# Turning the edge counts for the mask with transposing DMAs in place of GpSimd copies and TensorE products

## The chip, the cores and the metric

One core of a Trainium2 chip. The metric is device time in microseconds for one launch of the whole program, median of several runs. The kernel is written by hand with explicit semaphores: each engine (TensorE = PE, VectorE = DVE, ScalarE = ACT, GpSimd = POOL, SyncE = SP, which here only issues DMAs) runs its instructions in the written order and waits on semaphores.

## The reference

Two graph layers over 1024 nodes with 768 features and 16384 edges, each followed by a residual and a layer norm. The first is a graph attention network (8 heads, then 1 head), the second a two-step graph convolution. What the change touches belongs to the attention:

```
h = (x @ W1).reshape(n, 8, 768)                  # 1024 x 6144
alpha_s, alpha_d = h . a_src, h . a_dst          # per node and head
e = leaky_relu(alpha_s[src] + alpha_d[dst], 0.2)
m = segment_max(e, dst)                          # over the edges that arrive at dst
e = exp(e - m[dst]); alpha = e / (segment_sum(e, dst)[dst] + 1e-16)
out = segment_sum(h[src] * alpha, dst)           # then elu, a second such layer, and so on
```

The kernel is dense: it builds a matrix of edge counts `count[src, dst]` once and works with 1024x1024 matrices. For the maximum over arriving edges it needs a mask with the destination on the partitions: 0 where there is an edge, a large number where there is none.

## The kernel before

The layer's big product x @ W1 runs in 96 steps. QN = 12 column blocks q of 512 columns, each of NB = 8 node blocks b of 128 rows; step (q, b) has number n = 8q + b. A step is 18 products of TensorE (six blocks of features, each with three products of float32 split in a high and a low part, lines L41 to L43, moving 512 columns) into bank n % 6 of the PSUM. Banks 6 and 7 serve small work. Around a step (n):

- ACT copies the bank as the high part into `st[n % 4]` (L623, `main_high`). Before, it waits that the DMA which saved `st[n % 4]` four steps ago has landed (`h_saved`).
- DVE forms two logit sums from the bank (L979) and the low part of `st` (L1074), which counts `main_lo` up. TensorE's step n + 6 waits for `main_lo` of step n, since it takes the same bank.
- SP waits for `main_lo` and saves `st` to HBM (L445, 512 KB).
- ACT casts one block of the next W1 column block (`weights_high`, L591, in steps b = 1 to 6), POOL forms its low part `wl` (L574); TensorE's step (q + 1, 0) waits for all six.
- At b = 0 SP loads the weights of block q + 2 (L369, 1.5 MB), at b = 1 the vectors `a_bc` of block q + 1 (L373), each broadcast over the partitions.

The counts lie in `countT`, int16, [128 partitions of src, 8 blocks of src, 1024 dst], and are complete at the start of block q = 5. Then the mask is made, one block m of 128 destinations at a time, m = 0 to 7, two of them in each of q = 5, 6, 7, 8 (`BLOCK_AT` and `MASK_AT`):

- POOL copies `countT[:, :, block m]` to `staged[m % 2]` as bf16 (L570), two blocks ahead of its work on `wl` for that q. From m = 2 it waits for `staged_turned`.
- TensorE, after step (q, 1) for even m and (q, 5) for odd m, multiplies the eight 128x128 parts of `staged` with the unit matrix `ident_b`: the parts turned, in banks 6 and 7 (L1557). It waits for `staged_done` and for the mask before (`mask_done`), as the two banks are used again.
- ACT, after its work of step (q, 3) or (q, 7), waits for `staged_turned` and makes the mask by two Relu instructions that read banks 6 and 7 (L671).
- SP, one step later, saves that block of the mask to HBM (L377); DVE reads masks 0 to 3 for the first maxima after step (7, 1).

In the same stage SP handles vectors of logits and exponents: `row_bc` (L381), `expo_scratch` (L387, written as single values of 4 bytes) and `expo_bc` (L394). All the DMAs named here but a few small ones at the program's start run on SP's one hardware queue and its 16 DMA engines, in the order in which SP issues them. From q = 12 on the program goes to the attention sums (TensorE again in L41 to L43, `psum<-ph,hc`), the second layer, and the convolution.

Of the kernel before, what the change touches and what calls it, by code (L numbers as in the profile page):

```python
# [8 lines left out]
I16 = mybir.dt.int16  # L9
# [111 lines left out]
def graph_and_layers(nc, sem, put, psum, banks, t):  # L121
# [24 lines left out]
    junk = put("junk", 155648, [P, 2, CW], BF16)  # L146
    a_bc = [put(f"a_bc{i}", 157696 + 4096 * i, [P, 2, CW], F32) for i in range(2)]

    staged = [put(f"staged{i}", 165888 + 2048 * i, [P, NB, P], BF16) for i in range(2)]
    lane_sums = put("lane_sums", 169984, [P, N], F32)  # L150
    ident_b = put("ident_b", 179200, [P, P], BF16)
    mask_late = put("mask_late", 174080, [P, 2, N], BF16)
# [100 lines left out]
    count_full, count_out = sem("count_full"), sem("count_out")  # L253
    cols_full, cols_done = sem("cols_full"), sem("cols_done")
    x_turned, x_hi, x_lo = sem("x_turned"), sem("x_hi"), sem("x_lo")
    staged_done, staged_turned, deg_sum, mask_done = sem("staged_done"), sem("staged_turned"), sem("deg_sum"), sem("mask_done")
    mask_out = [sem(f"mask_out{i}") for i in range(2)]
    deg_step, root_done, dinv_done = sem("deg_step"), sem("root_done"), sem("dinv_done")
    dinvT_full, dinvT_done, dinv_out, many_full, many_done = (sem(n) for n in ("dinvT_full", "dinvT_done", "dinv_out", "many_full", "many_done"))
# [105 lines left out]
    with nc.Block() as block:  # L365
        @block.sync
        def _(sp):
# [7 lines left out]
            def save_mask(b):  # L375
                sp.wait_ge(mask_done, 2 * b + 2)
                sp.dma_start(mask_d[:, b * N:(b + 1) * N], mask_of(b)).then_inc(mask_out[b % 2], 16)  # L377

            def load_row(v):
                h = v % H  # L380
                sp.dma_start(row_bc[:, :], logits_d[h * NB:(h + 1) * NB, :].rearrange("b p -> (b p)").partition_broadcast(P)).then_inc(row_in, 16)  # L381
# [40 lines left out]
            for q in range(QN):  # L422
                for b in range(NB):
                    n = q * NB + b
                    if 1 <= q < QN - 1 and b == 1:
                        sp.wait_ge(part_sum, parts_before[q * NB])
                        load_vectors(q + 1)
                    if q < QN - 2 and b == 0:
                        if q == 0:
                            sp.wait_ge(w0_lo, FB)  # L430
                        else:
                            sp.wait_ge(w_lo, FB * q)
                        load_weights(q + 2)
                    if q == QN - 1 and b in (1, 2, 3):
                        if b == 1:
                            sp.wait_ge(staged_turned, NB)
                            sp.wait_ge(deg_sum, DEG_PARTS + 1)
                            for i in range(2):
                                sp.wait_ge(mask_out[i], 16 * NB // 2)
                        load_nodes(b - 1)  # L440
                    if n == STEPS - 1:
                        spread_exponents(1)
                    sp.wait_ge(main_lo, n + 1)
                    g = q * 4
                    sp.dma_start(h_d[g:g + 4, :, b, :, :].rearrange("g p k c -> p g k c"), st[n % 4][:, :, :, :].bitcast(F32)).then_inc(h_saved[n % 4], 16)  # L445
                    if (q, b - 1) in MASK_AT:
                        save_mask(MASK_AT[(q, b - 1)])
                    if b == 0 and (q - 1, NB - 1) in MASK_AT:
                        save_mask(MASK_AT[(q - 1, NB - 1)])
                    if (q, b) in SAVE_AT:  # L450
                        save_logits(SAVE_AT[(q, b)])
                    if (q, b) == (5, 1):
                        sp.wait_ge(count_out, NW)
                        sp.wait_ge(logits_out, 16)
                        load_row(0)
                    if (q, b) == (7, 4):
                        save_exponents(0)
                        load_row(1)
                    if (q, b) == (7, 7):
                        spread_exponents(0)  # L460
                    if (q, b) == (8, 4):
                        save_exponents(1)
                    if (q, b) == (10, 0):
                        sp.wait_ge(logits_out, 32)
                        load_row(2)
                    if (q, b) == (10, 4):
                        sp.wait_ge(dinvT_done, 1)
                        sp.dma_start(dinv_d, dinvT[:, :]).then_inc(dinv_out, 16)
# [77 lines left out]
        def _(pool):  # L546
# [9 lines left out]
            for q in range(QN - 1):  # L556
                if q in (2, 3):
                    pool.wait_ge(count_out, 8 * (q - 1))
                    for w in range(8 * (q - 2), 8 * (q - 1)):
                        pool.sem_clear(hot_ready[w % HOT_SEMS]).then_inc(hot_cleared, 1)  # L560
                        pool.sem_clear(hot_free[w % HOT_SEMS]).then_inc(hot_cleared, 1)
                if q == QM:
                    pool.wait_ge(count_out, NW)
                    for done in hot_ready + hot_free:
                        pool.sem_clear(done)
                for b in (2 * (q - QM), 2 * (q - QM) + 1):
                    if 0 <= b < NB:
                        if b >= 2:
                            pool.wait_ge(staged_turned, b - 1)
                        nc.gpsimd.tensor_copy(staged[b % 2][:, :, :], countT[:, :, b * P:(b + 1) * P]).then_inc(staged_done, 1)  # L570
                i = (q + 1) % 2
                for f in range(FB):
                    pool.wait_ge(w_hi, FB * (q + 1) + f + 1)
                    nc.gpsimd.tensor_tensor(wl[i][:, f, :], wr[i][:, f, :], wh[i][:, f, :].bitcast(F32), ALU.subtract).then_inc(w_lo, 1)  # L574
# [13 lines left out]
        def _(act):  # L588
# [54 lines left out]
            for q in range(QN):  # L643
                for b in range(NB):
# [18 lines left out]
                        weights_high(q + 1, b - 1)  # L663
                    if (q, b) in MASK_AT:
                        m = MASK_AT[(q, b)]
                        act.wait_ge(staged_turned, m + 1)
                        act.wait_ge(const_c, 3)
                        if m >= HNB + 2:
                            act.wait_ge(mask_out[m % 2], 16 * (m // 2))
                        for i in range(2):  # L670
                            nc.scalar.activation(mask_of(m)[:, i * 512:(i + 1) * 512], banks[6 + i][:, :], ACT.Relu, bias=unlinked[:, 0:1],  # L671
                                                 scale=NOT_LINKED).then_inc(mask_done, 1)
                    if (q, b) == (9, 6):
                        act.wait_ge(deg_step, 3)
# [786 lines left out]
        def _(pe):  # L1461
# [57 lines left out]
            for q in range(QN):  # L1519
                if q >= 1:  # L1520
                    pe.wait_ge(w_lo, FB * q)
                for b in range(NB):
# [23 lines left out]
                    if n + 1 in COUNT_AFTER:  # L1546
                        w = COUNT_AFTER[n + 1]
                        pairs = pe.value_load(range_i[w:w + 1, 1:2], min_val=FIRM // 2 + 1, max_val=EP)
                    if (q, b) in BLOCK_AT:
                        m = BLOCK_AT[(q, b)]  # L1550
                        pe.wait_ge(staged_done, m + 1)
                        if m == 0:
                            pe.wait_ge(logitT_done, 1)
                        else:
                            pe.wait_ge(mask_done, 2 * m)
                        for s in range(NB):
                            last = nc.tensor.matmul(banks[6 + s // 4][:, (s % 4) * P:(s % 4 + 1) * P], staged[m % 2][:, s, :], ident_b[:, :],  # L1557
                                                    start=True, stop=True)
                        last.then_inc(staged_turned, 1)
                    if (q, b) == (9, 0):  # L1560
                        pe.wait_ge(mask_done, 2 * NB)
                        pe.wait_ge(deg_sum, DEG_PARTS)
# [628 lines left out]
```

## Time and profile before

| | us |
|---|---|
| median of 3 runs | 1658.85 (1658.64 to 1658.88) |
| the profiled execution, its own time | 1656.4 |
| its span, first to last instruction | 1654.6 |
| PE busy | 1630.6 (99%), 7552 products |
| DVE busy | 1234.6 (75%) |
| ACT busy | 770.0 (47%) |
| POOL busy | 155.7 (9%) |
| SP's queue, share of 16 DMA engines | 52.9%, 267 MB |
| granted TensorE clock | 0.997 |

The profile is of one execution. "Busy" is the union of the instructions of an engine; a product of TensorE is shown as lasting 0.39 us though the next one starts 0.227 us after it, since they overlap in the array, so that starts are to be read, not lengths. SP's rows (SPq) are the times in which it issues a DMA, not the transfer; the transfer ends at its "landing". The stage of the change, q = 5 to 8, lies between 214 and 349 us of the span.

### The profile page before, as it was taken

The numbers are of one execution on the slowest core, as the hardware profiler recorded it, in microseconds if no ns is written. First come the engines' busy times: TensorE is split into PE (matmuls) and PEld (weight loads), VectorE is DVE, ScalarE is ACT, GpSimd is POOL, SyncE is SP. The second block draws the span as 40 slices with busy tenths as digits, with TensorE's granted clock in tenths as the row PEclk, the third lists the DMA queues.
The fourth block names the chain that finished last, engine by engine and source line by source line (L and its number), as shares of the span: only waits on it lengthen the run. The fifth ranks groups of instructions, "written<-read, shape, count | busy, mean of one in ns | idle before, by whom it ended". The sixth has DMA issues, their size and how long they took to land. (4 is left out here: it accounts for less than half of the span.)

```text
span 1654.6 us, 21905 instructions
## 1 busy us (share of the span) xinstructions
PE 1630.6 (99%) x7552; PEld 1368.2 (83%) x7552; DVE 1234.6 (75%) x2442; ACT 770.0 (47%) x1231; POOL 155.7 (9%) x126
## 2 busy tenths in 40 slices
PE   7999999999999999999999999999999999999998
PEld 6878888888878888888888888888888888989898
DVE  7877667655988788788778788877886668785447
ACT  3222223222565565456555555655564435644340
POOL 1211232322200000000000000000000001031003
PEclk9999999999999999999999999999999999999999
DMA  7444555984647475558647565754754447023222
GB/s 258 161 156 156 162 193 190 242 214 151 223 172 184 170 210 153 131 188 226 155 152 200 156 167 187 200 143 164 200 140 172 178 163 195 21 94 97 66 96 88
DMA packets 135331, 271.86 MB, mean 164 GB/s; under 512 B 24234, under 2 KB 83508, under 8 KB 122676
## 3 DMA queue, kind: packets, MB, share of 16 engines
q1 hardware_dynamic: 133968, 267.26, 52.9%
q0 software_dynamic: 1152, 3.15, 1.0%
q8 instruction: 63, 1.03, 0.3%
q14 instruction: 48, 0.39, 0.1%
q10 hardware_dynamic: 100, 0.03, 0.0%
HBM read 210.01 MB, written 60.40 MB: 163 GB/s over the span
## 5 line engine op out<-in xcount | busy, mean ns | idle before, releaser
L41 PE MATMUL psum<-ph,hc 128*128 128x512 f32 x768 | 299.4, 390 | 2.2 <-DVE pl L1040 1.2
L42 PE MATMUL psum<-pl,hc 128*128 128x512 f32 x768 | 298.8, 389 | 0.0
L43 PE MATMUL psum<-ph,hc 128*128 128x512 f32 x768 | 298.8, 389 | 0.0
L41 PE MATMUL psum<-wh,xTh 128*128 128x512 f32 x570 | 226.3, 397 | 0.4 <-issue 0.4
L42 PE MATMUL psum<-wl,xTh 128*128 128x512 f32 x570 | 222.2, 390 | 0.0
L43 PE MATMUL psum<-wh,xTl 128*128 128x512 f32 x570 | 222.0, 389 | 0.0
L979 DVE CUSTOM_DVE_ANT_0 junk<-psum,a_bc 128x512 bf16<-128x512 f32 (+1 forms) x256 | 129.8, 554 | 118.6 <-ACT st L623 108.6
L623 ACT CAST st<-psum 128x512 fp32r<-128x512 f32 x96 | 56.4, 588 | 296.2 <-PE psum L43 285.3
L41 PEld LDWEIGHTS psum<-ph,hc 128*128 128x128 f32 x768 | 144.2, 188 | 33.9 <-DVE pl L1040 2.1
L43 PEld LDWEIGHTS psum<-ph,hc 128*128 128x128 f32 x768 | 144.2, 188 | 30.0
L42 PEld LDWEIGHTS psum<-pl,hc 128*128 128x128 f32 x768 | 144.2, 188 | 29.7
L695 ACT ACTIVATE he<-mean,bias 128x512 f32<-128x512 f32 x96 | 69.6, 725 | 210.7 <-DVE mean L1129 210.7
L43 PE MATMUL psum<-w2h,hl 128*128 128x512 f32 x384 | 149.5, 389 | 0.0
L41 PE MATMUL psum<-w2h,hh 128*128 128x512 f32 x384 | 149.5, 389 | 0.0
L42 PE MATMUL psum<-w2l,hh 128*128 128x512 f32 x384 | 149.4, 389 | 0.0
L43 PEld LDWEIGHTS psum<-wh,xTl 128*128 128x128 f32 x570 | 107.0, 188 | 22.8
L41 PEld LDWEIGHTS psum<-wh,xTh 128*128 128x128 f32 x570 | 107.1, 188 | 22.2 <-issue 0.6
L42 PEld LDWEIGHTS psum<-wl,xTh 128*128 128x128 f32 x570 | 107.2, 188 | 20.8
L1129 DVE TENSOR_TENSOR mean<-psum,rden 128x512 f32<-128x512 f32 x96 | 65.8, 686 | 69.9 <-PE psum L43 69.8
L574 POOL TENSOR_TENSOR wl<-wr,wh 128x512 fp32r<-128x512 f32 x66 | 87.4, 1324 | 316.6 <-ACT wh L591 316.6
L687 ACT CAST w2h<-w2r 128x768 fp32r<-128x768 f32 x96 | 79.6, 829 | 73.4 <-PE psum L43 73.4
L641 ACT CAST ph<-pf 128x512 fp32r<-128x512 f32 x128 | 79.7, 622 | 70.1 <-DVE pf L1035 70.1
(285 smaller groups left out, 3116.7 us busy)
## 6 DMA issues: line engine op xcount, KB each, us to landing
hc<-h_scratch SPq DMA_DIRECT2D x96, 1024.0 KB, 5.3
h_scratch<-st SPq DMA_DIRECT2D x96, 512.0 KB, 3.2
w2r<-in_L_gnn_W SPq DMA_DIRECT2D x96, 384.0 KB, 6.8
wr<-in_L_gnn_W SPq DMA_DIRECT2D x12, 1536.0 KB, 8.6
gwr<-in_L_gnn_W SPq DMA_DIRECT2D x24, 384.0 KB, 3.4
row_bc<-logits_scratch SPq DMA_DIRECT2D x16, 512.0 KB, 12.9
expo_bc<-expo_scratch SPq DMA_DIRECT2D x16, 512.0 KB, 6.2
xr<-in_x SPq DMA_DIRECT2D x2, 1536.0 KB, 10.2
```

Of the source, the lines that this page charges most:

```text
L41: nc.tensor.matmul(out, sh, mh, start=first, stop=False, skip_group_check=not grouped)
L42: nc.tensor.matmul(out, sh, ml, start=False, stop=False, skip_group_check=not grouped)
L43: return nc.tensor.matmul(out, sl, mh, start=False, stop=last, skip_group_check=not grouped)
L574: nc.gpsimd.tensor_tensor(wl[i][:, f, :], wr[i][:, f, :], wh[i][:, f, :].bitcast(F32), ALU.subtract).then_inc(w_lo, 1)
L623: nc.scalar.copy(st[n % 4][:, :, 0, :], banks[n % 6][:, :].rearrange("p (g c) -> p g c", g=4)).then_inc(main_hi, 1)
L641: nc.scalar.copy(ph[v % 2][:, i, :], pf[:, i % 2, :]).then_inc(p_hi, 1)
L687: nc.scalar.copy(w2h[:, g % 3, :], w2r[:, g % 3, :]).then_inc(w2_hi, 1)
L695: nc.scalar.activation(he[:, g % 2, :], mean[:, g % 2, :], ACT.Exp, bias=b)
L979: nc.vector.tensor_tensor_reduce(out=junk[:, s % 2, 0:hi - lo], in0=banks[n % 6][:, lo:hi], in1=a_bc[q % 2][:, k, lo:hi], scale=1.0, scala ...
L1129: nc.vector.tensor_tensor(mean[:, g % 2, :], banks[6 + g % 2][:, :], rden[:, :], ALU.mult).then_inc(a_out, 1)
```

## The change

The turning is done by DMAs. After SP has issued the save of step (q, 1) or (q, 5) it issues eight transposing DMAs for block m, each of one 128x128 part of `countT` of 2-byte integers, straight from `countT` into `staged[m % 2]`, which is int16 now. The first batch waits for the last counts (`count_out`); from m = 2 a batch waits for the mask that last read this `staged`. The batch stands ahead of everything that SP had after that save. ACT waits for the landing of all eight (a semaphore for each of the two buffers) and reads `staged` in place of banks 6 and 7. POOL's eight copies and TensorE's 64 products are gone.

```diff
-    staged = [put(f"staged{i}", 165888 + 2048 * i, [P, NB, P], BF16) for i in range(2)]
+    staged = [put(f"staged{i}", 165888 + 2048 * i, [P, NB, P], I16) for i in range(2)]
...
-    staged_done, staged_turned, deg_sum, mask_done = sem("staged_done"), sem("staged_turned"), sem("deg_sum"), sem("mask_done")
+    staged_turned = [sem(f"staged_turned{i}") for i in range(2)]
+    deg_sum, mask_done = sem("deg_sum"), sem("mask_done")
...
+            def turn_counts(m):
+                if m == 0:
+                    sp.wait_ge(count_out, NW)
+                elif m >= 2:
+                    sp.wait_ge(mask_done, 2 * (m - 1))
+                for s in range(NB):
+                    sp.dma_start(staged[m % 2][:, s, :], countT[:, s, m * P:(m + 1) * P], transpose=True).then_inc(staged_turned[m % 2], 16)
...
-                            sp.wait_ge(staged_turned, NB)
+                            sp.wait_ge(mask_done, 2 * NB)
...
                     sp.dma_start(h_d[g:g + 4, :, b, :, :].rearrange("g p k c -> p g k c"), st[n % 4][:, :, :, :].bitcast(F32)).then_inc(h_saved[n % 4], 16)
+                    if (q, b) in BLOCK_AT:
+                        turn_counts(BLOCK_AT[(q, b)])
...
-                for b in (2 * (q - QM), 2 * (q - QM) + 1):
-                    if 0 <= b < NB:
-                        if b >= 2:
-                            pool.wait_ge(staged_turned, b - 1)
-                        nc.gpsimd.tensor_copy(staged[b % 2][:, :, :], countT[:, :, b * P:(b + 1) * P]).then_inc(staged_done, 1)
...
-                        act.wait_ge(staged_turned, m + 1)
+                        act.wait_ge(staged_turned[m % 2], 16 * NB * (m // 2 + 1))
...
-                            nc.scalar.activation(mask_of(m)[:, i * 512:(i + 1) * 512], banks[6 + i][:, :], ACT.Relu, bias=unlinked[:, 0:1],
+                            nc.scalar.activation(mask_of(m)[:, i * 512:(i + 1) * 512], staged[m % 2][:, 4 * i:4 * i + 4, :].rearrange("p s n -> p (s n)"), ACT.Relu, bias=unlinked[:, 0:1],
...
-                    if (q, b) in BLOCK_AT:
-                        m = BLOCK_AT[(q, b)]
-                        pe.wait_ge(staged_done, m + 1)
-                        if m == 0:
-                            pe.wait_ge(logitT_done, 1)
-                        else:
-                            pe.wait_ge(mask_done, 2 * m)
-                        for s in range(NB):
-                            last = nc.tensor.matmul(banks[6 + s // 4][:, (s % 4) * P:(s % 4 + 1) * P], staged[m % 2][:, s, :], ident_b[:, :],
-                                                    start=True, stop=True)
-                        last.then_inc(staged_turned, 1)
```

TensorE between step (5, 1) and step (5, 2), before (`wh_71` and `wl_73` are the high and low part of the weights):

```order
1142 L43 MATMUL psum<-wh_71,xTl 128x512
1143 L1557 MATMUL psum<-ident_b,staged_84 128x128 [waits logitT_done,staged_done]
1144 L1557 MATMUL psum<-ident_b,staged_84 128x128 x7
1145 L41 MATMUL psum<-wh_71,xTh 128x512 [waits main_lo]
1146 L42 MATMUL psum<-wl_73,xTh 128x512
```

And after, at the same place:

```order
1141 L42 MATMUL psum<-wl_73,xTh 128x512
1142 L43 MATMUL psum<-wh_71,xTl 128x512
1143 L41 MATMUL psum<-wh_71,xTh 128x512 [waits main_lo]
1144 L42 MATMUL psum<-wl_73,xTh 128x512
1145 L43 MATMUL psum<-wh_71,xTl 128x512
```

The two rows with `ident_b` and their waits have gone from between the steps; nothing has taken their place.

SP's queue from the save of step (5, 1) on, before:

```order
69 L445 DMA h_scratch<-st_78 128x4x256 [waits main_lo]
70 L381 DMA row_bc<-logits_scratch 128x1024 [waits logits_out,count_out]
71 L445 DMA h_scratch<-st_79 128x4x256 [waits main_lo]
72 L445 DMA h_scratch<-st_80 128x4x256 [waits main_lo]
73 L445 DMA h_scratch<-st_77 128x4x256 [waits main_lo]
74 L377 DMA mask_scratch<-mask_half 128x1024 [waits mask_done]
```

And after:

```order
69 L454 DMA h_scratch<-st_78 128x4x256 [waits main_lo]
70 L386 DMA_TRANSPOSE staged_84<-countT 128x128 [waits count_out]
71 L386 DMA_TRANSPOSE staged_84<-countT 128x128 x7
72 L390 DMA row_bc<-logits_scratch 128x1024 [waits logits_out,count_out]
73 L454 DMA h_scratch<-st_79 128x4x256 [waits main_lo]
74 L454 DMA h_scratch<-st_80 128x4x256 [waits main_lo]
```

Eight transposing DMAs stand behind the save of step (5, 1) and ahead of the load of `row_bc` and of the saves of the next steps.

ACT at step (5, 3), before:

```order
123 L623 CAST st_80<-psum 128x4x128 [waits h_saved3,main_full]
124 L591 CAST wh_70<-wr_68 128x512 [waits w_in0]
125 L671 ACTIVATE mask_half<-psum,unlinked 128x512 [waits const_c,staged_turned]
126 L671 ACTIVATE mask_half<-psum,unlinked 128x512
127 L623 CAST st_77<-psum 128x4x128 [waits h_saved0,main_full]
```

And after:

```order
123 L629 CAST st_80<-psum 128x4x128 [waits h_saved3,main_full]
124 L597 CAST wh_70<-wr_68 128x512 [waits w_in0]
125 L677 ACTIVATE mask_half<-staged_84,unlinked 128x512 [waits const_c,staged_turned0]
126 L677 ACTIVATE mask_half<-staged_84,unlinked 128x512
127 L629 CAST st_77<-psum 128x4x128 [waits h_saved0,main_full]
```

The mask stands where it stood, between the same neighbours; it waits for a landing now and reads `staged`.

## Rows read from the trace of the kernel before

**Rows 1.** The page's first part: busy us, share of the span, instructions
```profile
PE 1630.6 (99%) x7552; PEld 1368.2 (83%) x7552; DVE 1234.6 (75%) x2442; ACT 770.0 (47%) x1231; POOL 155.7 (9%) x126
```

**Rows 2.** Waits of PE, whole span: waited for, us in total, times, longest
```profile
PE psum L1465 <- DVE key_f L897: 5.0, 1, 5.0
PE psum L1533 <- ACT wh L591: 3.9, 1, 3.9
...
PE psum L41 <- DVE pl L1040: 1.2, 2, 0.7
```

**Rows 3.** Timeline of PE at boundaries of steps: start us, us, engine, line, operation
```profile
218.38 0.39 PE L41 MATMUL psum<-wh,xTh 128*128 128x512 f32 x1
...
222.47 0.62 PE L1557 MATMUL psum<-ident_b,staged 128*128 128x128 bf16 x8
222.90 0.47 PE L41 MATMUL psum<-wh,xTh 128*128 128x512 f32 x1
...
227.10 0.39 PE L41 MATMUL psum<-wh,xTh 128*128 128x512 f32 x1
...
231.18 0.39 PE L41 MATMUL psum<-wh,xTh 128*128 128x512 f32 x1
...
341.06 0.47 PE L41 MATMUL psum<-wh,xTh 128*128 128x512 f32 x1
```

**Rows 4.** Source view of L1557: all 64 products, first and last start
```profile
L1557 PE MATMUL psum<-ident_b,staged x64: 219/219/230, 222.5 to 341.0; 128*128 128x128 bf16 x64
```

**Rows 5.** Waits of ACT between 205 and 352 us
```profile
ACT st L623 <- PE psum L43: 100.8, 34, 3.5
ACT st L623 <- DMA h_scratch<-st: 3.8, 1, 3.8
```

**Rows 6.** Busy us of each engine, granted clock, DMA share and GB/s, by stretch
```profile
214.00:247.00 33.00, 33.00 (x159) 27.06 (x158) 19.43 (x46) 8.98 (x16) 10.05 (x9) 1.00 0.64 216
247.00:280.00 33.00, 33.00 (x158) 27.07 (x157) 22.22 (x45) 10.16 (x18) 8.97 (x8) 1.00 0.62 207
280.00:312.00 32.00, 32.00 (x154) 26.24 (x153) 24.67 (x73) 9.35 (x17) 9.25 (x8) 1.00 0.73 210
312.00:345.00 33.00, 33.00 (x158) 27.10 (x157) 21.80 (x60) 9.86 (x18) 10.27 (x8) 1.00 0.91 235
...
378.00:410.00 32.00, 32.00 (x145) 26.07 (x144) 15.39 (x62) 9.07 (x17) 6.99 (x6) 1.00 0.50 163
```

**Rows 7.** Timeline of SP's queue: when each DMA is issued, and how long that takes
```profile
225.22 0.38 SPq L445 DMA_DIRECT2D h_scratch<-st  x1
...
242.10 0.36 SPq L445 DMA_DIRECT2D h_scratch<-st  x1
...
306.65 0.96 SPq L387 DMA_DIRECT2D expo_scratch<-expo  x1
...
326.82 0.40 SPq L445 DMA_DIRECT2D h_scratch<-st  x1
```

**Rows 8.** Source view of L445, the saves of a step: issue to landing
```profile
DMA to landing us min/median/max: 2.9/3.2/14.4
```

**Rows 9.** The DMA view: a queue's packets, MB, share; issues' KB, us to landing
```profile
q1 hardware_dynamic: 133968, 267.26, 52.9%
...
h_scratch<-st SPq DMA_DIRECT2D x96, 512.0 KB, 3.2
...
expo_scratch<-expo SPq DMA_DIRECT2D x16, 4.0 KB, 13.3
```

**Rows 10.** Timeline of ACT, POOL and PE towards step (9, 0)
```profile
248.75 1.27 ACT L671 ACTIVATE mask_half<-psum,unlinked 128x512 bf16<-128x512 f32 x2
...
333.67 1.27 ACT L671 ACTIVATE mask_late<-psum,unlinked 128x512 bf16<-128x512 f32 x2
...
345.46 0.59 ACT L623 CAST st<-psum 128x512 fp32r<-128x512 f32 x1 [3.53 <-PE psum L43]
...
346.64 1.29 POOL L574 TENSOR_TENSOR wl<-wr,wh 128x512 fp32r<-128x512 f32 x1 [3.35 <-ACT wh L591]
...
349.34 0.39 PE L41 MATMUL psum<-wh,xTh 128*128 128x512 f32 x1
```

## The prediction

> **What bounds the kernel now.** I read the engines' busy times first: TensorE is busy 1630.6 of 1654.6 us [rows 1], so all its idle time together is 24 us. The view of its waits says where: 9 us of it at the very start, before the big product runs, and the rest in pieces of a microsecond or two in later stages [rows 2]. Between 214 and 345 us, where the change lies, the table by stretch has TensorE busy for every microsecond [rows 6]: no other engine or transfer holds it up there. Its timeline shows the beat: steps start at 227.10 and 231.18, that is 4.08 us for 18 products [rows 3]. Behind it, ACT waits 34 times for TensorE (100.8 us) and once, for 3.8 us, for a save that had not landed [rows 5]; DVE is busy for 60 to 77% of these stretches; the DMA engines for 62 to 91% [rows 6]. So what TensorE no longer does here is worth its full time, as long as nothing new makes it wait, and the candidate for that is the DMA side, which gets the work.
>
> **Part 1, TensorE loses 64 products: the gain.** The eight products of a block start at 222.47 and the next step at 222.90, so they hold the stream for 0.43 us [rows 3]. The step behind them is slower too: 222.90 to 227.10 is 4.20 us against the 4.08 of the step after it. Checked from the other side, step (5, 1) with its block takes 218.38 to 222.90 = 4.52 us, which is 4.08 + 0.44. Together 0.44 + 0.12 = 0.56 us for a block. There are 8 blocks, the first at 222.5 us and the last at 341.0 [rows 4], and the last one ends the same way, with a first product that shows 0.47 us at 341.06 [rows 3]. 8 x 0.56 = **4.5 us**. The pairs of waits that go with them cost nothing now: they are within the 0.43.
>
> In the Trainium skill, "VectorE: DVE Perf Modes", section "The three transpose paths", a turn of 128x128 in bf16 takes 390 ns on TensorE. The trace disagrees: in a running stream eight of them take 0.43 us, some 54 ns each, as they overlap. By the page's figure the gain would be 64 x 0.39 = 25 us; TensorE has no such time to give in these rows.
>
> **Does the gain reach the end?** Only if no engine behind TensorE sets the pace later. The stretch 378 to 410 us has DVE busy for 15.4 of 32 us [rows 6], so DVE is not behind when the blocks are over: everything up to there follows TensorE's steps and moves up with them. The two waits of the attention's first sums for DVE's `pl` (1.2 us, [rows 2]) hang on work that starts after those steps, and move as a whole. I take all 4.5 us.
>
> **Part 2, POOL loses eight copies.** Nobody waits for POOL's copies and POOL itself is busy 9 to 10 of 33 us [rows 6]. Worth nothing.
>
> **Part 3, SP issues 64 more DMAs.** No transposing DMA is in this trace, so its issue is bounded by other issues: 0.36 us for a save, 0.96 us for the pile of small pieces of `expo_scratch` [rows 7]. I take 0.6 us, between them, since a save is one regular block as a 128x128 part is. Eight take 4.8 us (2.9 to 7.7), every fourth step, that is once in 16.3 us, in which SP's other issues take 3 to 4 us: the queue keeps up even at 0.96. Queued behind the batch on SP are `row_bc`, the saves of the next steps, and at (7, 5) and (8, 1) nothing else that is urgent. How late may a save be? The save of step (5, 1) is issued at 225.22, 2.75 us after TensorE ended the step at 222.47, and lands 3.2 us later [rows 3, 7, 8], in all 6 us. ACT needs the buffer when step n + 4 ends, 16.3 us after step n: 10 us to spare. And TensorE needs the bank of step n + 4 not before step n + 10, 5 steps or 20.4 us after it, of which ACT and DVE take 2.75: 17.6 more. So a save may be **28 us** late in all before TensorE waits. SP would have to hold up by more than 1.6 us per transfer (16.3 less 3.5, by eight) before such a lag even grew from block to block.
>
> **Part 4, 64 transfers on the DMA engines.** Each moves 32 KB. By bytes, at the pace of a save (512 KB in 2.9 us [rows 8]), it is 0.18 us of all 16 engines. By packets: SP's queue moved 133968 packets in 52.9% of 16 engines' 1654.6 us, on average 0.105 us of one engine for a packet [rows 9]; 128 rows of 256 bytes are 128 packets, 8 for each engine, 0.84 us. I take 0.4 us, nearer to the bytes, as these packets are an eighth of the average packet's 2 KB. All 64 take 26 us (12 to 54). What is free in the four stretches: 0.36 x 33 + 0.38 x 33 + 0.27 x 32 + 0.09 x 33 = 36 us [rows 6]. Even the upper value overfills that by 18 us at most, which is under the 28 us of slack. On the path: nothing.
>
> In "DMA: Bandwidth & Descriptors" of the Trainium skill, section "Latency and other measured facts", a DMA transpose runs at 261 GB/s. By that a transfer is 0.13 us and the batch is hidden all the more. No run of the kernel before can show it.
>
> **Part 5, ACT's new wait.** For a block at (q, 5) the save is issued at 242.10, the last of eight transfers at about 242.5 + 4.8 = 247.3, and it lands 2.9 us later at 250.2; ACT comes to the mask at 248.75 [rows 7, 10]. So ACT will wait about 1.5 us (0 to 5), in time that it spends waiting for TensorE anyway. Queued behind this wait are the casts of the next steps and, at (q, 3), the casts of the next weights: POOL ends the last low part at 346.64 + 1.29 = 347.93 and TensorE starts step (9, 0) at 349.34, a margin of 1.4 us; between the mask (over at 334.94) and the cast at 345.46 ACT has 10.5 us with 2.4 us of work in it, 8.1 free [rows 10]. So a landing may come **9.5 us** after ACT is ready at (q, 3). The tightest block is at (8, 1), where the DMA engines are busiest: issued from 326.82 + 0.40 on, with a landing as late as the longest of all saves, 14.4 us [rows 7, 8], it comes at 341.6, 8 us after ACT's 333.67. Just within. The mask's own two instructions read another memory and another type; I cost that at nothing, ACT being under a third busy [rows 6].
>
> **Sum.** -4.5 + 0 + 0 + 0 + 0. The profiled execution took 1656.4 us (span 1654.6), 2.45 below the median of 1658.85; the span should be 1650.1 and the median **1654.4 us**.
>
> **The rivals.**
> (a) The DMA engines become the bound, **slower**. It decides at a cost c of one transfer, in us of all 16 engines, where 64 c is over the free 36 plus the slack of 28: c = 1.0. The mechanism: saves land ever later, ACT waits for `h_saved`, then TensorE for `main_lo`. If a turned part is written in as many packets again as it is read in, c is 2 x 0.84 = 1.7, and 64 x 1.7 - 64 = 45 us are lost, less 4.5. Between 1.0 and 1.7, at 1.35, it is 22.4 - 4.5 = +18: **1677 us** (1655 to 1699). For it: 91% busy in the last stretch and one wait for a save already [rows 5, 6]. Against: it needs packets dearer than the queue's average. Far worse is possible by one row: `expo_scratch` moves 4 KB in 1024 pieces in 13.3 us [rows 9]; if each element went by itself, 16384 of them would take 213 us a part, and the program over 13000 us.
> The same page of the Trainium skill (VectorE, "The three transpose paths") says to turn 128x128 on TensorE where PSUM will do, with 1309 ns for the DMA. Taken as c it would give 83.8 - 64 - 4.5 = +15 us, 1674; taken as a latency, it changes nothing.
> (b) The mask's landing at (q, 3) is over 9.5 us late, and the weights' low part with it, so that TensorE waits at (q + 1, 0), up to four times. At 11 us late in three of them it is 3 x 1.5 = 4.5 us: the gain is eaten, **1658.9 us**. For it: the margin of 1.5 us at (8, 1). Against: the other three are freer.
> (c) TensorE gains but waits it out at the first attention sums, where it waits for DVE today [rows 2]: **1658.6 us**. Against: DVE's half-idle stretch before [rows 6].
> (d) The 0.12 us in the step behind is not the products' doing and stays: 3.5 us, **1655.4 us**, still a gain, within the forecast's own range.
>
> **How the numbers follow.** Forecast with (d) 0.65; (a) 0.16 and its extreme 0.02; (b) 0.12; (c) 0.05. A measurement of this kernel tells a change of some 0.2% (3.3 us) from none; 4.5 us is 0.27%, so even the likeliest case is not far over the bound. Faster by over 0.2%: 0.65 less a little for (d) with a small loss, 0.62. Slower: (a), 0.18. Within 0.2%: (b), (c) and that little, 0.20. The range: from 1653.6, some overlap gained besides, to the forecast (0.64), over (b) and (c) (0.17) into the lower half of (a), up to 1670 us. The likeliest case alone spans 1653.6 to 1655.6.
>
> **What would show each step.** Right: no idle time of PE from 214 to 345 us, every step there 4.08 us, step (9, 0) starting near 344.9; ACT waiting for `staged` by 1 to 8 us a block; issues near 0.6 us; DMA share up by some 0.2 in the four stretches. (a) shows as PE waiting for DVE's `main_lo` and ACT for saves; (b) as PE waiting at the start of blocks 6 to 9 for POOL; (c) as longer waits for `pl` near 455 us. The prediction is wrong if a transposing transfer holds SP for over 1.6 us or the DMA engines for over 1.0 us.

## The result, and the profile after

The changed kernel takes 1688.28 us (1688.04 to 1689.38, 4 runs) against 1658.74: the ratio is 1.018 (1.016 to 1.020), 29.5 us slower where 4.5 us less were forecast. The profiled execution has a span of 1686.2 us, 31.6 over that of before.

TensorE was busy in every microsecond of this stage before [rows 6] and now waits in it. Its waits over the whole span, with what it waited for, us in total, times and the longest:

```profile
PE psum L41 <- POOL wl L580: 14.8, 3, 6.9
PE psum L1559 <- ACT mask_late L677: 11.0, 1, 11.0
PE psum L1471 <- DVE key_f L903: 5.0, 1, 5.0
```

The third row is the old wait at the start [rows 2]. The first two are new, 25.8 us: three waits for the low part of the next weights, at the starts of q = 7, 8 and 9, and one for the last mask in step (9, 0). Neither engine named is the cause. All waits from 205 to 385 us lead further back:

```profile
POOL wl L580 <- ACT wh L597: 125.3, 14, 19.9
ACT mask_late L677 <- DMA staged<-countT: 64.4, 4, 18.3
...
ACT mask_half L677 <- DMA staged<-countT: 40.5, 4, 14.0
```

POOL waits for ACT, and ACT waits for the landings of the turned counts, eight times, 105 us in all. The stretches that answer to [rows 6]:

```profile
214.00:247.00 33.00, 33.00 (x147) 27.37 (x146) 20.84 (x46) 9.29 (x17) 7.74 (x6) 1.00 0.67 220
247.00:280.00 33.00, 32.21 (x143) 26.34 (x141) 17.98 (x38) 9.73 (x19) 6.06 (x5) 1.00 0.64 182
280.00:312.00 32.00, 30.42 (x134) 25.20 (x135) 22.39 (x62) 5.12 (x10) 5.33 (x5) 1.00 0.65 196
312.00:345.00 33.00, 27.51 (x111) 22.21 (x110) 14.09 (x49) 9.64 (x18) 7.54 (x6) 0.90 0.96 195
345.00:378.00 33.00, 16.73 (x65) 13.00 (x63) 15.35 (x43) 4.81 (x9) 3.73 (x3) 0.82 0.92 156
```

TensorE is still full at first: ACT lags from its first mask on, but the lag is invisible in TensorE until the work prepared ahead of it is used up, and shows from 279 us on, at the start of q = 7. The last column but two is the granted clock, as a share of 2.4 GHz: its mean falls to 0.82 in the stretch in which TensorE idles most.

Why are the landings late? The source view of the transposing DMAs (issue time in ns, least, median, most) and SP's timeline around the second batch:

```profile
L386 SPq DMA_TRANSPOSE staged<-countT x64: 1219/1234/2667, 225.1 to 372.5; - x64
```

```profile
243.13 0.36 SPq L454 DMA_DIRECT2D h_scratch<-st  x1
243.53 11.59 SPq L386 DMA_TRANSPOSE staged<-countT  x8
255.17 1.13 SPq L454 DMA_DIRECT2D h_scratch<-st  x2
...
262.34 0.73 SPq L454 DMA_DIRECT2D h_scratch<-st  x1
263.11 1.93 SPq L386 DMA_TRANSPOSE staged<-countT  x1
```

One transfer holds SP for 1.22 us at least and 1.23 in the median; a batch, with its gaps, holds it for 11.6 us here and 10.8 to 11.7 in all eight. And ACT, around the same time:

```profile
246.61 0.59 ACT L629 CAST st<-psum 128x512 fp32r<-128x512 f32 x1 [2.83 <-PE psum L43]
256.26 1.34 ACT L677 ACTIVATE mask_half<-staged,unlinked 128x512 bf16<-128x512 int16 x2 [9.06 <-DMA staged<-countT]
...
275.38 1.33 ACT L677 ACTIVATE mask_half<-staged,unlinked 128x512 bf16<-128x512 int16 x2 [11.35 <-DMA staged<-countT]
...
294.18 1.33 ACT L677 ACTIVATE mask_half<-staged,unlinked 128x512 bf16<-128x512 int16 x2 [13.97 <-DMA staged<-countT]
```

Read the starts of the masks: 256.26, 275.38, 294.18, one every 19 us, where TensorE makes four steps in 16.3. And the waits grow: 9.06, 11.35, 13.97 (the first, at 237.53 us, was 6.14). So the masks no longer follow TensorE but a beat of their own, which closes on itself: SP issues a batch (11.6 us, 243.53 to 255.12), the last part lands about a microsecond later, ACT makes the mask and then the casts that it owes, SP saves those steps, and behind the save of step (6, 1), at 262.34, the next batch begins at 263.11. The later masks start at 313.85, 336.95, 356.20 and 378.24: 19 to 20 us apart, but 22 to 23 for blocks 5 and 7, the two that stand behind a DMA of `expo_scratch`.

### The profile page after: what moved, and what is told of

Its sections match the earlier page's. It is cut to its first block and busy times, and to the rows that moved or that the text cites. A ratio compares the mean times of both kernels' runs of the same rounds, so it can differ in the third digit from the quotient of the medians.

```text
span 1686.2 us, 21825 instructions
## 1 busy us (share of the span) xinstructions
PE 1634.4 (97%) x7488; PEld 1370.8 (81%) x7488; DVE 1231.8 (73%) x2442; ACT 768.6 (46%) x1231; POOL 144.1 (9%) x118
## 3 DMA queue, kind: packets, MB, share of 16 engines
q1 hardware_dynamic: 144208, 269.36, 53.7%
## 5 line engine op out<-in xcount | busy, mean ns | idle before, releaser
L41 PE MATMUL psum<-wh,xTh 128*128 128x512 f32 x570 | 228.6, 401 | 15.2 <-POOL wl L580 14.8
## 6 DMA issues: line engine op xcount, KB each, us to landing
xr<-in_x SPq DMA_DIRECT2D x2, 1536.0 KB, 10.2
```

Source lines behind the costliest of these rows:

```text
L41: nc.tensor.matmul(out, sh, mh, start=first, stop=False, skip_group_check=not grouped)
```

## The experiments

Each ran beside the kernel before on one chip; there it measured 1657.0 us (first four), 1658.1 (next four) and 1657.7 (last two), so ratios are what is compared.

### The gain alone

```diff
@@ tensor: the eight products of a block (cut) @@
-                        pe.wait_ge(staged_done, m + 1)
...
-                            last = nc.tensor.matmul(banks[6 + s // 4][:, (s % 4) * P:(s % 4 + 1) * P], staged[m % 2][:, s, :], ident_b[:, :],
-                                                    start=True, stop=True)
-                        last.then_inc(staged_turned, 1)
@@ scalar: the mask, from POOL's copies @@
-                        act.wait_ge(staged_turned, m + 1)
+                        act.wait_ge(staged_done, m + 1)
```

Not shown here: ACT reads `staged` in place of banks 6 and 7, and POOL's copies and one wait of SP go by `mask_done` in place of `staged_turned`.

> The kernel before with only the turning left out: TensorE's 64 products are gone, POOL's copies stay, ACT makes the mask from the copied counts unturned (so the turning itself is left out and the mask is of the wrong orientation). No transposing DMA. My theory of part 1 (0.44 us of products and 0.12 us in the step behind, eight times): 1654.3 us, and every step from 214 to 349 us 4.08 us long. The rival, that the 0.12 us is not the products' doing: 1655.2 us. The rival, that the gain is given back at later waits: 1658.6 us.

Measured: 0.9973 (0.9964 to 0.9983), 1652.7 against 1657.0 us. Step (5, 1) and step (9, 0) on its timeline:

```profile
217.76 0.39 PE L41 MATMUL psum<-wh,xTh 128*128 128x512 f32 x1
...
344.24 0.39 PE L41 MATMUL psum<-wh,xTh 128*128 128x512 f32 x1
```

Between them lie 126.48 us, 31 steps of 4.08; before, the same steps take 218.38 to 349.34 = 130.96 [rows 3, 10]. The difference is 4.48 us, as forecast, the 0.12 us in the step behind included. At the end of the program 4.3 of it are left (1657.0 less 1652.7).

### The landings without a waiter

```diff
@@ after.py (cut) @@
-                    sp.wait_ge(mask_done, 2 * (m - 1))
+                    sp.wait_ge(staged_turned[m % 2], 16 * NB * (m // 2))
...
-                        act.wait_ge(staged_turned[m % 2], 16 * NB * (m // 2 + 1))
...
-                            nc.scalar.activation(mask_of(m)[:, i * 512:(i + 1) * 512], staged[m % 2][:, 4 * i:4 * i + 4, :].rearrange("p s n -> p (s n)"), ACT.Relu, bias=unlinked[:, 0:1],
+                            nc.scalar.activation(mask_of(m)[:, i * 512:(i + 1) * 512], countT[:, m, 512 * i:512 * (i + 1)], ACT.Relu, bias=unlinked[:, 0:1],
```

SP's batch no longer waits for a mask either, only for the landings of the batch two before.

> The changed kernel, all 64 transposing DMAs issued at their places, but the mask is made from the counts unturned (the use of the turned counts is left out), so that ACT waits for no landing; the landings are waited for only at the end of the stage. Theory A (the loss comes from a loop: SP holds a batch for over 10 us, ACT waits for its landing before it goes on with the casts, and SP's next batch waits behind saves that wait for these casts): without the wait the loop is open and SP needs some 14 of 16.3 us a block, so 1654 to 1656 us. Theory B (the DMA engines are overfull, or transposes slow the other transfers): the transfers are the same, so it stays near 1685 us. Theory C (the saves queued behind the batch come too late for ACT by themselves): 1660 to 1680 us, with ACT waiting for saves.

Measured: 1.0050 (1.0035 to 1.0066), 1666.3 us. Theory B falls as the main cause, as the same transfers cost 9 us in place of 29.5; but theory A does not give the whole either. A wait of TensorE over the whole span, ACT's longest kind of wait from 205 to 385 us, and ACT's timeline at one of them:

```profile
PE psum L41 <- POOL wl L582: 11.4, 3, 7.6
```

```profile
ACT st L631 <- DMA h_scratch<-st: 70.1, 19, 7.7
```

```profile
271.89 0.59 ACT L631 CAST st<-psum 128x512 fp32r<-128x512 f32 x1 [2.54 <-PE psum L43]
...
278.15 0.59 ACT L631 CAST st<-psum 128x512 fp32r<-128x512 f32 x1 [5.16 <-DMA h_scratch<-st]
```

SP's timeline at the same place has why:

```profile
261.23 13.61 SPq L386 DMA_TRANSPOSE staged<-countT  x8
274.89 2.24 SPq L456 DMA_DIRECT2D h_scratch<-st  x3
```

Three saves stood behind 13.6 us of transposing DMAs, and with them the buffers `st`. ACT comes late to its casts by that, and TensorE waits for the weights' low part. That is theory C, a second path beside the first: 9 us over the kernel before, 13.5 over e1, though nobody waits for the turned counts.

### Fewer transfers in a batch

```diff
@@ after.py (cut); 4 in one kernel, 6 in the other @@
-                for s in range(NB):
+                for s in range(4):
```

> The changed kernel with four in place of eight transposing DMAs a block; the first half of a mask block is made from their result, the second from the counts unturned (half of the turning is left out). Theory A: a turn of the loop takes about 1.27 us times the count of DMAs plus 8.8 us, so 13.9 us with four, under the 16.3 us of four steps: no growing lag, 1654 to 1656 us. Theory B with half the transfers: 1665 to 1672 us.

> The same with six transposing DMAs a block, the mask made from six turned parts, two of them read twice (a quarter of the turning is left out). Theory A: the loop takes 6 x 1.27 + 8.8 = 16.4 us against 16.3, at the edge: a lag that hardly grows, 1655 to 1661 us. Theory B, in proportion to the transfers: 1677 to 1682 us.

Measured: 1.0047 (1.0032 to 1.0062) with four, 1.0102 (1.0087 to 1.0118) with six, against 1.018 with eight; in us against 1657.0: +7.0 and +16.5. Both miss theory A's times by 8 us and more, and both lie below theory B's; the traces say which part of A holds. Its beat is right for the first blocks: with four, TensorE has no wait up to step (9, 0); with six, ACT waits 3.7 to 5.4 us for the landings of blocks 0 to 4, a lag that hardly grows, where it grew from 6.1 to 14.5 with eight. At block 5, behind the first DMA of `expo_scratch` and the load of `row_bc`, it jumps to 12.65. With four, what is left is one wait of TensorE:

```profile
PE psum L1559 <- ACT mask_late L677: 7.3, 1, 7.3
```

and SP's queue at the last block, with four:

```profile
339.57 0.88 SPq L396 DMA_DIRECT2D expo_scratch<-expo  x1
340.50 0.89 SPq L454 DMA_DIRECT2D h_scratch<-st  x1
341.43 10.23 SPq L386 DMA_TRANSPOSE staged<-countT  x4
```

Four transfers that take 5.2 to 7.4 us in the other seven blocks take 10.2 behind the DMA of `expo_scratch`, the one with 1024 pieces of 4 bytes [rows 9]. TensorE's small products at the end of step (9, 0) wait for the last mask, which ACT makes after its work of step (8, 7). Before, TensorE's own turning made that mask early enough. With six, that wait is 9.9 us, and one of 4.1 us for `wl` comes with it.

### The whole batch three steps earlier

```diff
@@ after.py @@
+    EARLY_AT = {divmod(NB * QM + 1 + 4 * m - 3, NB): m for m in range(NB)}
...
-                    if (q, b) in BLOCK_AT:
-                        turn_counts(BLOCK_AT[(q, b)])
+                    if (q, b) in EARLY_AT:
+                        turn_counts(EARLY_AT[(q, b)])
```

> The changed kernel with each batch of eight issued three steps earlier, so that a landing has five steps (20 us) before ACT needs it; nothing is left out. If ACT's wait for the landings were all of the loss: 1653 us (the gain of e1 in full). If the saves queued behind a batch are a second path of their own, as in e2: SP is still held for over 10 us at a time, ACT waits for saves, and it stays near e2, 1661 to 1667 us.

Measured: 1.0053 (1.0038 to 1.0069), 1667.2 us: the second expectation, at its upper end. ACT waits for no landing of the turned counts, but for saves, as in e2:

```profile
ACT st L630 <- DMA h_scratch<-st: 79.4, 19, 10.8
```

TensorE waits 9.5 us for `wl`, in two waits. So more time for the landing is not enough; the next runs break up the batch.

### Two transfers a step

```diff
@@ after.py @@
+    SPREAD_FROM = NB * QM + 1 - 3
...
-                for s in range(NB):
+                for s in range(2 * j, 2 * j + 2):
...
-                    if (q, b) in BLOCK_AT:
-                        turn_counts(BLOCK_AT[(q, b)])
+                    if 0 <= n - SPREAD_FROM < 4 * NB:
+                        turn_counts((n - SPREAD_FROM) // 4, (n - SPREAD_FROM) % 4)
```

> The changed kernel with two transposing DMAs after each save in place of eight after every fourth, from three steps before the batch's old place up to it; nothing is left out. SP is held 2.5 of 4.08 us a step, so no save should be late. What is left is the last block: its last two DMAs are issued at step (8, 5), behind the DMA of expo_scratch, land some 12 us later, and TensorE waits for the last mask in step (9, 0) as in e3_k4: 1658 to 1661 us. If overfull DMA engines are what matters, it stays over 1665 us.

Measured: 1.0090 (1.0074 to 1.0105), 1672.7 us. ACT waits only 0.7 us for a save, but the rest was mis-sized: it waits 44 us for landings at masks 4 to 7, and TensorE 2.9 us for `wl` and 10.7 us for the last mask. By the expectation a time over 1665 us speaks for overfull DMA engines; the next run, with the same transfers, decides against that. It is the same kernel with the start two steps earlier:

```diff
-    SPREAD_FROM = NB * QM + 1 - 3
+    SPREAD_FROM = NB * QM + 1 - 5
```

> The same, two steps earlier still, so that the last block's DMAs are issued at steps (8, 0) to (8, 3), ahead of expo_scratch; nothing is left out. If the two paths (saves behind a batch, the last landing behind expo_scratch) are all of it: no waits of TensorE from 214 to 349 us and the time of e1, 4 to 4.5 us under the kernel before, 1653 us. If a third cause exists, it shows here: 1656 us and more.

Measured: **0.9977 (0.9967 to 0.9986)**, 1654.4 against 1658.1 us, faster than both kernels. That is 3.7 us less than the kernel before, where e1 has 4.3. TensorE has one wait of 1.0 us left from 214 to 349 us, for `wl` at (9, 0), and ACT waits for no landing of the turned counts: the last DMAs of block 5 now stand ahead of the first DMA of `expo_scratch`, and those of block 7 ahead of the second. SP's queue now alternates:

```profile
303.37 0.58 SPq L457 DMA_DIRECT2D h_scratch<-st  x1
303.99 2.77 SPq L389 DMA_TRANSPOSE staged<-countT  x2
306.81 0.58 SPq L457 DMA_DIRECT2D h_scratch<-st  x1
```

Two more rows, ACT's waits from 205 to 385 us and the stretch in which the DMA engines were fullest before:

```profile
ACT st L632 <- DMA h_scratch<-st: 38.7, 11, 9.9
```

```profile
312.00:345.00 33.00, 33.00 (x148) 27.31 (x146) 20.79 (x52) 10.27 (x18) 8.12 (x5) 1.00 1.08 230
```

Saves still come late, by up to 9.9 us, but TensorE is full: that fits the slack which the prediction saw behind a late save, as long as nothing else draws on it. And the profile's share of the DMA engines goes up to 1.08 while TensorE does not wait, so that a share near 1 does not mean that there is no room left.

### Fewer, wider transfers

```diff
@@ after.py @@
-    staged = [put(f"staged{i}", 165888 + 2048 * i, [P, NB, P], I16) for i in range(2)]
+    staged = put("staged", 180224, [P, HNB, NB, P], I16)
+    WIDE_FROM = (38, 55)
...
-                    sp.dma_start(staged[m % 2][:, s, :], countT[:, s, m * P:(m + 1) * P], transpose=True).then_inc(staged_turned[m % 2], 16)
+                for s in range(2 * j, 2 * j + 2):
+                    sp.dma_start(staged[:, :, s, :], countT[:, s, half * HALF:(half + 1) * HALF], transpose=True).then_inc(staged_turned[half], 16)
```

The sixteen are issued behind the saves of steps (4, 6) to (5, 1) and (6, 7) to (7, 2), ahead of both DMAs of `expo_scratch`.

> The turning by 16 transposing DMAs of 128x512 in place of 64 of 128x128, two a step, eight for masks 0 to 3 and eight for masks 4 to 7; nothing is left out. If what holds SP goes by the instruction, one takes about 1.3 us and the time is that of e1 or less, 1653 us; if it goes by the bytes, one takes 4.9 us, SP is held 9.8 us a step for eight steps in all, and the time is 1656 to 1670 us.

Measured: **0.9976 (0.9966 to 0.9985)**, 1654.1 us, and no wait of TensorE in the stage. The source view (issue in ns):

```profile
L387 SPq DMA_TRANSPOSE staged<-countT x16: 1247/1690/2727, 214.1 to 302.7; - x16
```

A transfer of four times the bytes holds SP for 1.25 us at least and 1.69 in the median, where the small one has 1.22 and 1.23 in the changed kernel and 1.15 and 1.31 in e5b. What holds SP goes mostly by the instruction at these sizes, not by the bytes.

### One DMA moved

In e5_spread and in the changed kernel, the write of the second set of exponents goes from step (8, 4) to (9, 2), out of the way of the last block:

```diff
-                    if (q, b) == (8, 4):
+                    if (q, b) == (9, 2):
                         save_exponents(1)
```

> e5_spread with one thing moved: SP writes the second set of exponents (the 4 KB in single values of expo_scratch) after step (9, 2) in place of (8, 4), so that it no longer stands ahead of the last block's last two transposing DMAs; nothing is left out. If that DMA is what made the last mask late in e5_spread: TensorE waits at most 1 us in step (9, 0), its clock stays up, and the time is 4 us under the kernel before, 1653 to 1655 us. If the last block is late by its place alone: 1660 us and more.

> The changed kernel with the same one thing moved, its batches of eight as they were; nothing is left out. The loop of batch, landing, casts and saves stays, so TensorE still waits for the weights' low parts, but the last mask comes some 8 us earlier: 1676 to 1682 us, against 1688 for the changed kernel. If the loop did nothing: 1654 us. If expo_scratch did nothing: 1688 us.

Measured: 1.0030 (1.0018 to 1.0043), 1662.7 us, for the spread one (1.0090 without the move), and 1.0154 (1.0137 to 1.0171), 1683.3 us, for the changed kernel (1.018 without). Both lie in between and miss their expected ranges, the second by 1.3 us. The wait for the last mask in the spread one fell from 10.7 to 1.3 us:

```profile
PE psum L41 <- POOL wl L583: 2.5, 1, 2.5
...
PE psum L1562 <- ACT mask_late L680: 1.3, 1, 1.3
```

The move takes 10 of the 14.6 us that e5_spread loses against the kernel before, and 4 of the changed kernel's 29.5. The rest of e5_spread's loss is lag from the blocks before: ACT still waits 10.9 and 11.5 us for blocks 5 and 6, and the first set of exponents, with the load of `row_bc`, still stands ahead of the end of block 5. Those two were not moved, so that their share is argued and not shown. The loop, in the changed kernel, stays what it was: 14.9 us of waits for `wl`, against 14.8. What the move did there can be read at the last block, with the second DMA of `expo_scratch` out of the way:

```profile
362.50 10.79 SPq L386 DMA_TRANSPOSE staged<-countT  x8
```

```profile
374.41 1.33 ACT L677 ACTIVATE mask_late<-staged,unlinked 128x512 bf16<-128x512 int16 x2 [13.09 <-DMA staged<-countT]
```

The mask starts 1.1 us after the batch has been issued (373.29). In the changed kernel that takes 4.6 us at this block (362.87 + 10.81 = 373.68, mask at 378.24), 4.9 at block 5, and 1.1 to 2.0 at the other six. The issue of the batch is as long in both; the landing is what comes late. TensorE's wait for the last mask falls from 11.0 to 7.3 us.

## Why the prediction was wrong

**Part 1 was right**: 4.48 us measured in e1 against 4.5, of which 4.3 reach the end. **Part 2** is borne out: e1 keeps POOL's copies, e5b and e7 do without them and are no faster.

**Part 3 failed, in its size and in its test.** I put a transposing issue between a save (0.36 us) and the pile of small pieces (0.96 us) and took 0.6. It is 1.23 us in the median, 1.40 with the gaps (89.6 us for 64): outside the bounds that I drew from plain DMAs. The row that I took as the upper end was not a bound. It was not even the dearest plain issue; two others in the same stage of the trace of before are dearer:

```profile
319.99 1.10 SPq L369 DMA_DIRECT2D wr<-in_L_gnn_W  x1
...
323.07 2.12 SPq L377 DMA_DIRECT2D mask_scratch<-mask_late  x1
```

And the point of decision was wrong too. I asked whether SP's own work fits into four steps (under 1.6 us a transfer), which it does with 1.40: the two signs that I named for the prediction being wrong (over 1.6 us on SP, over 1.0 us on the DMA engines) did not come, and it was wrong all the same. But the batch does not run beside the rest: the batch, its landing, ACT's mask, the owed casts and the next save are one chain that ends in the next batch. Its length is 19 us against 16.3, so the lag grows by 2.3 to 2.9 us a block over the first four (6.14, 9.06, 11.35, 13.97). With four transfers the chain comes to 13.9 us and the lag does not grow, with six to 16.4 and it hardly grows (e3). I had worked out the room for a late save and the room for a late landing each by itself, and not asked whether the late one feeds the other.

**Part 4, the DMA engines, held in its conclusion.** For my 0.4 us for a transfer: SP's queue took 53.7% of 16 engines' 1686.2 us, with

```profile
q1 hardware_dynamic: 144208, 269.36, 53.7%
```

against 52.9% of 1654.6 [rows 9], 905.5 - 875.3 = 30 us more for 64 transfers, 0.47 each, waits in the queue included. The same sum gives 26 us in e5b (54.5% of 1653.1) and 12 in e9 (52.8% of 1681.3), so that it is known as 0.2 to 0.5 us and no better. The packets came out at 160 for a transfer (144208 less 133968, by 64), where I had counted 128 and rival (a) 256. Rival (a), the only one on the slower side, named the wrong resource: its time of 1677 is the nearest to the measured one, by luck, but its mechanism was not at work, since e5b and e7 move the same counts through the same engines and gain. My 36 us of free time were read from the share of the DMA engines, which is no measure of room, as its 1.08 in e5b shows.

**Part 5 failed, by Part 3's term and by omissions.** ACT's wait was forecast at 0 to 8 us; it was 6 to 18. A batch of 11.6 us in place of 4.8 adds 6.8 us to my 1.5, and the last landing 1.1 us behind the batch, where I took 2.9, takes 1.8 off: 6.5 us, and 6.1 were measured at block 0. The rest, in the later blocks, is the growing lag. My own limit of 9.5 us for a landing at (q, 3) was passed from block 2 on, which waits 11.35. For the block at (8, 1) I had also let the longest landing, 14.4 us, begin with the first of the eight issues: with the 4.8 us of the others it comes to 12.7 us, over that limit on my own numbers, and not "just within" it. Of those that wait for ACT I named the casts of the saves and of the weights. I did not name TensorE's small products in step (9, 0), which wait for all masks; `mask_done` stood in the code ahead of them. The last block also stands behind a DMA of `expo_scratch`, which is 3.7 of the 11.0 us of TensorE's wait there (e9); I had the row with its 13.3 us [rows 9] in hand, and used it for a far-fetched extreme in place of asking what it would be in front of. SP's and ACT's timelines there:

```profile
361.01 0.88 SPq L396 DMA_DIRECT2D expo_scratch<-expo  x1
361.93 0.89 SPq L454 DMA_DIRECT2D h_scratch<-st  x1
362.87 10.81 SPq L386 DMA_TRANSPOSE staged<-countT  x8
```

```profile
378.24 1.33 ACT L677 ACTIVATE mask_late<-staged,unlinked 128x512 bf16<-128x512 int16 x2 [17.22 <-DMA staged<-countT]
```

Rival (b), waits at the starts of the blocks for the weights' low part, was the mechanism of 14.8 of the 25.8 us. I priced it at 4.5, from single late blocks and not from a lag that adds up.

**Where the 31.6 us of span went.** -4.5 of products; +14.8 and +11.0 of waits; and a cost that the prediction left out, TensorE's clock. Stretches of the changed kernel (the last column but two is the granted clock as a share of 2.4 GHz):

```profile
372.00:376.00 4.00, 0.00 (x0) 0.00 (x0) 0.00 (x0) 0.00 (x0) 0.00 (x0) 0.65 1.10 107
376.00:380.00 4.00, 0.38 (x2) 0.38 (x2) 0.00 (x0) 1.76 (x3) 0.00 (x0) 0.50 1.15 327
380.00:384.00 4.00, 4.00 (x17) 3.87 (x18) 1.91 (x5) 0.04 (x1) 0.00 (x0) 0.50 1.05 378
```

After 11 us without work TensorE runs its next products at half the clock, 1.2 GHz, one every 0.43 us in place of 0.227, into step (9, 1); the waits of 5.5 us ahead of step (8, 0) and of 6.9 ahead of step (9, 0) were followed by the same. Read from the starts of steps, less the waits: step (8, 0) takes 2.6 us more than its 4.08, step (9, 0) 3.9 and step (9, 1) 1.7 more than before, in all some 8 us. The sum is -4.5 + 25.8 + 8.2 = 29.5. The other 2 us of span are about what the two profiled executions differ by: that of before was 2.3 us under its median, that of the changed kernel 0.2. Of them 1.5 are seen as waits for `gyl` in the convolution. All runs but e3_k6 (0.2 us) have them, e1 among them, and the trace of before has none, so that they are no cost of the DMAs; where they come from is open.

How the loss divides between the loop and the queued saves cannot be said by adding: they share SP. The queued saves alone are enough for 9 us (e2 and e4, where ACT waits for no landing). The loop has no run of its own with eight transfers and no saves behind them; what shows it is its beat, the fit with four and six, and e9, where it keeps its 14.9 us. The gain came only where the batches were broken up and the last DMAs of blocks 5 and 7 stood ahead of those of `expo_scratch` (e5b, e7).

## What to carry to other kernels

Before moving work to a DMA queue, ask how long one instruction holds the issuing engine, and what stands behind it there: here the DMA engines had room, and SP had room on average, but not for eight transposing DMAs in a row. Ask also what stands ahead: a transfer behind a slow one lands late. If the engine that waits for the result also feeds the queue that makes it, lay all steps of one turn end to end and compare the sum with the beat of the bound engine; a room worked out for each wait alone says nothing on a lag that adds up. The cure leaves nothing out: two transfers a step, early enough to stand ahead of the slow DMAs (e5b), or fewer and wider ones, as early (e7). They keep 3.7 and 4.0 us of the gain.

## What was not expected of the hardware

- A transposing DMA from SBUF to SBUF holds the queue of SP for 1.15 to 1.22 us at least (median 1.23 in the changed kernel) for 128x128 elements of 2 bytes, and for 1.25 us at least (median 1.69, e7) for 128x512, where a save of 512 KB holds it for 0.36 in the median. The quickest landed 2.3 us after the start of its issue, the median one of the changed kernel after 3.7.
- The page "VectorE: DVE Perf Modes" of the Trainium skill, section "The three transpose paths", gives 1309 ns for a transpose of 128x128 in bf16 by DMA. In these traces that is near to the 1.23 us for which SP is held, and neither the latency (2.3 us at least) nor what the DMA engines spend (0.2 to 0.5 us). I had read it as one of the latter two.
- A DMA of 4 KB in 1024 pieces of 4 bytes delays what is behind it on the queue. With it in front, a batch of eight landed 4.6 us after its last issue, without it after 1.1 (e9). In e3_k4 four issues took 10.2 us behind it and 5.2 to 7.4 elsewhere; with eight in a batch the issues themselves took no longer.
- Idle times of 5 to 11 us cost TensorE its clock for the steps that follow: some 8 us here on top of 25.8. In e8 a wait of 2.5 us ahead of step (9, 0) was already followed by products at half the clock, one of 3.1 us ahead of step (8, 0) in e2 was not; what decides is not shown.
